# Grouped attention of layer one: transposes two rounds behind, value products as three rounded ones, ACT exchanges the query halves

## What is computed

```python
def _L0_attn_b_ref(hidden_states, Wq, Wkr, Wdk, Wupk, Wupv, Wo):
    q = (hidden_states @ Wq.T).reshape(bsz, q_len, N_HEADS, HEAD_DIM).transpose(0, 2, 1, 3)
    ...
    q = q * cos + _rotate_half(q) * sin
    k = k * cos + _rotate_half(k) * sin
    ...
    c_kv = hidden_states @ Wdk.T
    k_c = c_kv @ Wupk.T
    v = (c_kv @ Wupv.T).reshape(bsz, q_len, KV_HEADS, HEAD_DIM).transpose(0, 2, 1, 3)
    ...
    scores = jnp.einsum('bhqd,bhkd->bhqk', q, k) * scale
    scores = jnp.where(causal[None, None], scores, jnp.asarray(-1000000000.0, dt))
    attn = jax.nn.softmax(scores, axis=-1)
    out = jnp.einsum('bhqk,bhkd->bhqd', attn, v)
    return out.transpose(0, 2, 1, 3).reshape(bsz, q_len, N_HEADS * HEAD_DIM) @ Wo.T
```

## Time and profile before

| what | before |
|---|---|
| median of 3 runs | 2343.27 us |
| the profiled execution, its time | 2351.52 us |
| its span, first to last instruction | 2349.8 us |
| mean granted TensorE clock | 0.952 |
| PE, DVE, ACT, POOL busy | 90%, 60%, 46%, 36% |
| grouped attention, projections | 364 to 526 us |
| grouped attention, loop | 526 to 1276 us |

### The profile page before, as it was taken

The page is one execution under the profiler, slowest core; times in us unless marked ns, Lnnn a source line. Parts: engine busy times, 40 slices in busy tenths (PEclk is TensorE's granted clock), DMA queues, the critical chain, the costliest instruction groups (busy, mean ns, idle before and its releaser), DMA issues. The chain is left out here.

```text
span 2349.8 us, 33208 instructions
## 1 busy us (share of the span) xinstructions
PE 2125.6 (90%) x11408; PEld 1456.4 (62%) x11408; DVE 1406.4 (60%) x2597; ACT 1082.5 (46%) x2627; POOL 835.4 (36%) x1060
## 2 busy tenths in 40 slices
PE   5999988878999999999997879999999986899988
PEld 3333356656777777777765656777777674554457
DVE  5788464326656566556554636666666555657756
ACT  4677543214444444444443635555555433335553
POOL 0000101545344444444431035455555313246621
PEclk8999888989999999999999979999999987989999
DMA  3000022751011111111011144444333201543310
GB/s 112 1 1 1 4 90 84 153 128 41 25 53 37 36 54 32 41 54 32 23 41 36 62 103 108 108 108 105 88 98 78 61 23 58 160 91 68 72 33 37
DMA packets 113587, 149.48 MB, mean 64 GB/s; under 512 B 40127, under 2 KB 53567, under 8 KB 111246
## 3 DMA queue, kind: packets, MB, share of 16 engines
q1 hardware_dynamic: 65422, 109.08, 16.4%
q0 software_dynamic: 48000, 38.28, 7.1%
HBM read 86.39 MB, written 27.26 MB: 48 GB/s over the span
## 5 line engine op out<-in xcount | busy, mean ns | idle before, releaser
L1851 POOL TENSOR_TENSOR attn0b_probs<-attn0b_probs,attn0b_recip 128x128 f32<-128x128 f32 (+3 forms) x256 | 192.4, 772 | 223.4 <-DVE attn0b_recip L2090 223.3
L2482 POOL TENSOR_TENSOR attn1a_probs<-attn1a_probs,attn1a_recip 128x128 f32<-128x128 f32 (+3 forms) x256 | 178.9, 720 | 234.8 <-DVE attn1a_recip L2665 234.2
L2538 ACT ACTIVATE attn1a_probs<-attn1a_scores,attn1a_negmax 128x128 f32<-128x128 f32 (+3 forms) x256 | 132.7, 523 | 175.4 <-DVE attn1a_negmax L2651 174.2
L1957 ACT ACTIVATE attn0b_probs<-attn0b_scores,attn0b_negmax 128x128 f32<-128x128 f32 (+3 forms) x256 | 132.6, 523 | 150.0 <-DVE attn0b_negmax L2083 148.8
L1965 ACT ACTIVATE attn0b_probsT<-attn0b_turned 128x128 f32<-128x128 f32 (+3 forms) x128 | 56.0, 437 | 243.3 <-PE attn0b_turned L2231 242.9
L2244 PE MATMUL attn0b_out<-attn0b_probsT,attn0b_v_now 128*128 128x512 f32 x320 | 153.9, 612 | 11.4 <-DVE attn0b_probsT L2097 11.4
L1440 DVE TENSOR_REDUCE attn0a_negmax<-attn0a_by_query 128x2 f32<-128x1024 f32 x128 | 151.9, 1219 | 11.7 <-PE attn0a_by_query L1557 11.7
L2651 DVE TENSOR_REDUCE attn1a_negmax<-attn1a_scores 128x2 f32<-128x256 f32 (+3 forms) x128 | 105.4, 824 | 71.4 <-PE attn1a_scores L2840 71.4
L2083 DVE TENSOR_REDUCE attn0b_negmax<-attn0b_scores 128x2 f32<-128x256 f32 (+3 forms) x128 | 104.8, 819 | 46.9 <-PE attn0b_scores L2220 46.9
L37 PE MATMUL attn0b_aux<-attn0b_wo_hi,attn0b_oT_hi 128*128 128x512 f32 x256 | 125.6, 490 | 1.4 <-DVE attn0b_oT_lo L2101 1.4
L2852 PE MATMUL attn1a_turned<-ident_f,attn1a_probs 128*128 128x128 f32 x640 | 116.1, 280 | 8.7 <-DVE attn1a_probsT L2659 7.3
(11 more groups left out here) (507 smaller groups left out, 6121.2 us busy)
## 6 DMA issues: line engine op xcount, KB each, us to landing
pre<-in_b_o SPq DMA_DIRECT2D x16, 1024.0 KB, 5.3
attn1a_qT<-attn1a_stage SPq DMA_DIRECT2D x128, 128.0 KB, 2.4
attn1a_qT<-attn1a_stage SPq DMA_DIRECT2D x64, 256.0 KB, 3.8
pre<-in_b_q SPq DMA_DIRECT2D x8, 1024.0 KB, 6.1
pre<-in_b_kv SPq DMA_DIRECT2D x5, 1024.0 KB, 7.1
attn0b_vals<-attn0b_v_out SPq DMA_DIRECT2D x16, 256.0 KB, 5.0
attn0b_keys_hi<-attn0b_part_hi POOLq DMA_DIRECT2D x32, 128.0 KB, 4.9
attn0b_keys_lo<-attn0b_part_lo POOLq DMA_DIRECT2D x32, 128.0 KB, 7.6
```

The lines of the kernel that those rows point to most:

```text
L1851: pool.tensor_tensor(x, x, recip[:, r % 2, e:e + 1].broadcast_to([P, (qt + 1) * P]), ALU.mult).then_inc(s_scaled, 1)
L1957: act.activation(probs[:, r % 2, e, 0:width], scores[r % 2][:, e, 0:width], ACT.Exp, bias=negmax[:, r % 2, e:e + 1], accum_out=sums[:, r % ...
L2482: pool.tensor_tensor(x, x, recip[:, r % DEEP, e:e + 1].broadcast_to([P, (qt + 1) * P]), ALU.mult).then_inc(s_scaled, 1)
L2538: act.activation(probs[:, r % DEEP, e, 0:width], scores[r % 2][:, e, 0:width], ACT.Exp, bias=negmax[:, r % 2, e:e + 1], accum_out=sums[:, ...
```

## The change

- The probabilities, their sums and reciprocals have three buffers (`DEEP`). PE transposes a round two rounds after its scores: in the pass over `at` the first round of tile at-1 behind the query projection, and its second round at the end. The value product is that of tile at-2, the output product that of tile at-3.
- Both heads of a round are transposed and then leave together: `turned_hi` (ACT) writes the rounded part of both, `turned_lo` (DVE) the rest. The value product is three rounded matmuls per key block (`mm3`), with values in hi and lo.
- The projections therefore store the values in hi and lo: a subtraction (`value_lo`, DVE) and a store of twice the size; the loop loads both. In SP's order the second half of the values stands before the output weights of the next turn.
- Queries: ACT copies the two halves of the bank crosswise into `q_swap` (two buffers), DVE multiplies the bank by the cosine and `q_swap` by the sine table, whose halves are exchanged at loading: two multiplications for three. The bank is free for the output product after the cosine.
- Orders: on DVE `add_output` (of tile at-4) is first in a tile, `output_lo` and `query_lo` are last; on ACT `output_hi` and `query_hi` are last; on POOL both scalings of a tile and `add_rotated` are in the same pass. The query projection waits for the addition of tile at-4. The output weights are split at the end of the third tile of a turn.

```diff
...
-    FIRST, LAST = -LEAD, TILES_ALL + 1
+    DEEP = 3
+    FIRST, LAST = -LEAD, TILES_ALL + 3
...
-            v_out = take_sb("v_out", [P, 2, DIM])
-        q_cos, q_sin = n.sb("q_cos", [P, 2, SEQ]), n.sb("q_sin", [P, 2, SEQ])
+            v_out = take_sb("v_out", [P, 2, 2, DIM], F32R)
+        q_cos, q_swap = n.sb("q_cos", [P, 2, SEQ]), n.sb("q_swap", [P, 2, SEQ])
...
-        v_now = n.sb("v_now", [P, BATCH, QT, HD])
+        v_hi, v_lo = n.sb("v_hi", [P, BATCH, QT, HD], F32R), n.sb("v_lo", [P, BATCH, QT, HD], F32R)
...
-        probs = n.sb("probs", [P, 2, PAIRS, SEQ])
-        probsT = n.sb("probsT", [P, 2, QT, G, P])
+        probs = n.sb("probs", [P, DEEP, PAIRS, SEQ])
+        probsT_hi = [n.sb(f"probsT_hi{i}", [P, QT - 1 + i, G, P], F32R) for i in range(2)]
+        probsT_lo = [n.sb(f"probsT_lo{i}", [P, QT - 1 + i, G, P], F32R) for i in range(2)]
...
-        negmax, sums, recip = [n.sb(k, [P, 2, PAIRS]) for k in ("negmax", "sums", "recip")]
+        negmax = n.sb("negmax", [P, 2, PAIRS])
+        sums, recip = n.sb("sums", [P, DEEP, PAIRS]), n.sb("recip", [P, DEEP, PAIRS])
...
-        q_raw = n.sb("q_raw", [P, SEQ])
...
-                sp.wait_ge(s_v, at + 1)
-                sp.dma_start(vals[t, :, bass.ts(half, DIM)], v_out[:, at % 2, :]).then_inc(s_vals[at % 2], 16)
+                sp.wait_ge(s_vlo, at + 1)
+                sp.dma_start(vals[t, :, :, bass.ts(half, DIM)], v_out[:, at % 2, :, :].bitcast(F32)).then_inc(
+                    s_vals[at % 2], 16)
...
+                load_values(i, 1)
+                if i + 1 < TURNS:
...
-                load_values(i, 1)
...
         def _(pool):
...
             def add_rotated(c):
-                pool.wait_ge(s_rope, 3 * c + 3)
-                pool.tensor_tensor(q_cos[:, c % 2, :], q_cos[:, c % 2, :], q_sin[:, c % 2, :], ALU.add).then_inc(s_qadd, 1)
+                pool.wait_ge(s_rope, 2 * c + 2)
+                pool.tensor_tensor(q_cos[:, c % 2, :], q_cos[:, c % 2, :], q_swap[:, c % 2, :], ALU.add).then_inc(s_qadd, 1)
...
             def scale(r):
...
-                    x = probs[:, r % 2, e, 0:(qt + 1) * P]
-                    pool.tensor_tensor(x, x, recip[:, r % 2, e:e + 1].broadcast_to([P, (qt + 1) * P]),
+                    x = probs[:, r % DEEP, e, 0:(qt + 1) * P]
+                    pool.tensor_tensor(x, x, recip[:, r % DEEP, e:e + 1].broadcast_to([P, (qt + 1) * P]),
...
-                if 0 <= at <= TILES_ALL and 2 * at - 1 >= 0:
-                    scale(2 * at - 1)
-                if 1 <= c <= HEADS_ALL:
-                    add_rotated(c - 1)
...
+                if c < HEADS_ALL:
+                    add_rotated(c)
+                if 0 <= at < TILES_ALL:
+                    scale(2 * at + 1)
...
-                if r >= 2:
-                    act.wait_ge(s_turned, 2 * (r - 2) + e + 1)
-                    act.wait_ge(s_recip, r - 1)
-                act.activation(probs[:, r % 2, e, 0:width], scores[r % 2][:, e, 0:width], ACT.Exp,
-                               bias=negmax[:, r % 2, e:e + 1], accum_out=sums[:, r % 2, e:e + 1]).then_inc(s_exp, 1)
-            def copy_second(r):
+                if r >= DEEP:
+                    act.wait_ge(s_turned, r - DEEP + 1)
+                    act.wait_ge(s_recip, r - DEEP + 1)
+                act.activation(probs[:, r % DEEP, e, 0:width], scores[r % 2][:, e, 0:width], ACT.Exp,
+                               bias=negmax[:, r % 2, e:e + 1], accum_out=sums[:, r % DEEP, e:e + 1]).then_inc(s_exp, 1)
+            def turned_hi(r):
...
-                act.wait_ge(s_turned, 2 * r + 2)
+                act.wait_ge(s_turned, r + 1)
...
-                act.activation(probsT[:, at % 2, 0:qt + 1, 2 * p + 1, :], turned[:, 1, 0:qt + 1, :], ACT.Copy).then_inc(
-                    s_copied[1], 1)
+                act.activation(of_pair(probsT_hi, at, qt, p), turned[:, :, 0:qt + 1, :], ACT.Copy).then_inc(s_pthi, 1)
...
             def output_hi(at):
...
-            def query_out(c):
+            def swap_query(c):
...
-                if c >= 1:
-                    act.wait_ge(s_rope, 3 * c)
-                act.activation(q_raw[:, :], query_bank(c), ACT.Copy).then_inc(s_raw, 1)
+                if c >= 2:
+                    act.wait_ge(s_qadd, c - 1)
+                for into, of in ((slice(0, 64), slice(64, P)), (slice(64, P), slice(0, 64))):
+                    act.activation(q_swap[into, c % 2, :], query_bank(c)[of], ACT.Copy).then_inc(s_swap, 1)
...
             for at in range(FIRST, LAST + 1):
...
-                if at >= 2:
-                    output_hi(at - 2)
+                    for stored in s_keys:
+                        act.wait_ge(stored, 16 * 4 * 8)
+                if 0 <= 2 * at - 3 < ROUNDS:
+                    turned_hi(2 * at - 3)
...
-                    query_out(c)
-                if 1 <= at <= TILES_ALL:
-                    copy_second(2 * at - 1)
-                if 1 <= c <= HEADS_ALL:
-                    query_hi(c - 1)
+                    swap_query(c)
+                if 0 <= 2 * at - 2 < ROUNDS:
+                    turned_hi(2 * at - 2)
...
-                    copy_second(2 * at)
-                if at >= 0 and at % TILES == 1 and at // TILES < TURNS:
+                if 0 <= at - 2 < TILES_ALL:
+                    output_hi(at - 2)
+                if 1 <= c <= HEADS_ALL:
+                    query_hi(c - 1)
+                if at >= 0 and at % TILES == 2 and at // TILES < TURNS:
...
+            def value_lo(x):
+                dve.wait_ge(s_vhi, x + 1)
+                dve.tensor_tensor(v_out[:, x % 2, 1, :], proj[PROJ["V", x] % NB], v_out[:, x % 2, 0, :].bitcast(F32),
+                                  ALU.subtract).then_inc(s_vlo, 1)
...
+                    value_lo(7)
...
-                        dve.wait_ge(s_tables, 64)
+                        dve.wait_ge(s_tables, 80)
...
+                        value_lo(f[1] - 1)
...
+                elif f[1] >= 8:
+                    value_lo(f[1])
...
             def output_weights_lo(i, j):
...
-            def rotate(c):
-                dve.wait_ge(s_raw, c + 1)
+            def rotate_cos(c):
+                dve.wait_ge(s_swap, 2 * c + 2)
...
-                x = q_raw[:, :]
-                dve.tensor_tensor(q_cos[:, c % 2, :], x, cos_q[:, :], ALU.mult).then_inc(s_rope, 1)
-                for into, of in ((slice(0, 64), slice(64, P)), (slice(64, P), slice(0, 64))):
-                    dve.tensor_tensor(q_sin[into, c % 2, :], x[of], sin_q[of, :], ALU.mult).then_inc(s_rope, 1)
+                dve.tensor_tensor(q_cos[:, c % 2, :], query_bank(c), cos_q[:, :], ALU.mult).then_inc(s_rope, 1)
+            def rotate_sin(c):
+                dve.tensor_tensor(q_swap[:, c % 2, :], q_swap[:, c % 2, :], sin_q[:, :], ALU.mult).then_inc(s_rope, 1)
...
             def query_lo(c):
...
             def invert(r):
...
-                if r >= 2:
-                    dve.wait_ge(s_scaled, PAIRS * (r - 1))
-                dve.reciprocal(recip[:, r % 2, :], sums[:, r % 2, :]).then_inc(s_recip, 1)
-            def copy_first(r):
+                if r >= DEEP:
+                    dve.wait_ge(s_scaled, PAIRS * (r - DEEP + 1))
+                dve.reciprocal(recip[:, r % DEEP, :], sums[:, r % DEEP, :]).then_inc(s_recip, 1)
+            def turned_lo(r):
...
-                dve.wait_ge(s_turned, 2 * r + 1)
-                if at >= 2:
-                    dve.wait_ge(s_pv, at - 1)
-                dve.tensor_copy(probsT[:, at % 2, 0:qt + 1, 2 * p, :], turned[:, 0, 0:qt + 1, :]).then_inc(s_copied[0], 1)
+                dve.wait_ge(s_pthi, r + 1)
+                dve.tensor_tensor(of_pair(probsT_lo, at, qt, p), turned[:, :, 0:qt + 1, :],
+                                  of_pair(probsT_hi, at, qt, p).bitcast(F32), ALU.subtract).then_inc(s_ptlo, 1)
...
             def output_lo(at):
...
-                if at >= 2:
-                    output_lo(at - 2)
+                    for stored in s_keys:
+                        dve.wait_ge(stored, 16 * 4 * 8)
+                if 0 <= at - 4 < TILES_ALL:
+                    add_output(at - 4)
...
+                if 0 <= 2 * at - 3 < ROUNDS:
+                    turned_lo(2 * at - 3)
...
-                if 1 <= at <= TILES_ALL:
-                    copy_first(2 * at - 1)
+                if c < HEADS_ALL:
+                    rotate_cos(c)
...
-                    rotate(c)
+                    rotate_sin(c)
+                if 0 <= 2 * at - 2 < ROUNDS:
+                    turned_lo(2 * at - 2)
...
+                if 0 <= at - 2 < TILES_ALL:
+                    output_lo(at - 2)
...
-                if at >= 2:
-                    add_output(at - 2)
-                if 0 <= at < TILES_ALL:
-                    copy_first(2 * at)
-                if at >= 0 and at % TILES == 1 and at // TILES < TURNS:
+                if at >= 0 and at % TILES == 2 and at // TILES < TURNS:
...
+            def query_out_of_bank(c):
+                pe.wait_ge(s_rope, 2 * c + 1)
```

(44 more changed lines are left out.)

24 lines of the change are left out of this document (14 added, 10 removed).

## The result

The changed kernel takes 2353.8 us (median of 20 runs, 2348.06 to 2365.01). The kernel before, run beside it, takes 2348.8 us (20 runs, 2342.29 to 2355.12). The ratio is 1.0025, with a 95% interval of 1.0014 to 1.0036: slightly slower, where 2329 against 2343 had been forecast (ratio 0.994). The profiled executions have spans of 2349.8 and 2358.7 us. The two executions differ by 3.6 us before the block begins and by 3.5 us the other way behind it, in code that the change doesn't touch; so what is to be explained lies between the first matmul of the block and its last. One more thing to keep in mind: the profiled execution of the changed kernel took 2360.4 us, 6.6 above its median, at a mean granted clock of 0.938 where the median of its 20 runs is 0.941; that of the kernel before lies 2.7 us above its median.

A forecast was written before the change was run, and what follows sets the result against it. PE, busy 90% of the span, was taken as the bound, through its work and waits. Terms -27.5 + 7.5 + 5 - 3 + 4 = -14 us on the 2343.3 median gave 2329.3 us (forecast case 2315 to 2337, full range 2305 to 2353).

The forecast's parts named there:

- Part 1: Value product on PE: a key block falls from 0.86 to 0.69 us, 160 blocks, 27.5 us saved.
- R4: Rival: three matmuls cost three quarters of the old block, 0.645 us, saving 34.4 us; 2322 us, chance 0.08.
- Part 2: Middle of the attention: DVE stays at 386 us, ACT goes from 284 to about 345; neither becomes the bound.
- Part 3: Middle: later transposes remove 20 waits on POOL's scaling, about 20.5 us; new waits cost 28 us; +7.5 us.
- (a): A tile's first transposes wait for DVE's subtraction: 2.3 us, covered by 2.8 us of query projection, 0.5 to spare.
- (b): Query projection waits for the output addition queued behind DVE's four output-weight subtractions: 2.7 us, once per turn.
- (c): DVE's query part meets POOL's second scaling: 0.3 to 0.5 us in three tiles, 1.3 us a turn.
- 89 to 91.5: Sign: a turn of eight tiles takes 90.2 us, and the forecast is wrong outside this range in us.
- Part 4: Ends of the attention: last tiles' waits about 17 us against 12.0, +5; first queries sooner, -3 us.
- Part 5: Projections: doubled value stores cost 0 to 13 us, taken as 4; DVE's 16 subtractions lie in idle time.
- R2: Rival: gain used up, stores delay keys 13 us (+9), meetings cost 0.9 us each (+7); 2345 us, chance 0.20.

The follow-up runs named there:

- x2: Changed kernel, with PE doing 16 unused matmuls into a free bank before the late query projection in each turn's fourth tile; 2342.81 us, ratio 0.9979.
- x1: Changed kernel, with DVE's four output-weight subtractions moved from a turn's third tile to the middle of its fourth, behind the output addition; 2328.99 us, ratio 0.9912.
- x4: Changed kernel, with the output-weight subtractions spread over a turn's fourth tile and the output addition moved to the tile's end, before the query part; 2310.93 us, ratio 0.9844.
- b1: Kernel before, with DVE's value subtraction and the doubled value store added in the projections, old loop; 2356.43 us, ratio 1.0027.
- b3: Kernel before, with each value block stored twice (same copy) and no added DVE or ACT work; 2359.59 us, ratio 1.0047.
- b2: Kernel before, with DVE's 16 value subtractions alone added in the projections, bytes stored unchanged; 2354.7 us, ratio 1.0036.
- x7: Changed kernel, with POOL's scaling of the probabilities cut to one column per head, order and waits kept; 2330.28 us, ratio 0.9923.
- x5: x4, with DVE subtracting the transposed probabilities ahead of the maximum in the last five tiles; 2300.86 us, ratio 0.9798.
- x6: x5, with four buffers instead of two for the key parts in the projections; 2286.12 us, ratio 0.9732.

## Why the prediction was wrong

The forecast's sum was -14 us, and the two traces show +8.8 in the block (the medians +5.0). By the accounting above, against the forecast's terms, the step that failed most is one that the sum doesn't have: it takes PE's once-a-turn wait as its own length, and nothing for the clock behind it.

- **Part 1, the value product: right.** 0.69 us a block, as the rows show, and PE's work in the loop is 24 us less against 27.5. A part of it lies where the forecast didn't look: the output product behind the value product takes 2.73 us instead of 3.14, and the value product itself hardly gets shorter in the mean. The steps of the earlier trace rows ran into the output product, so the sum came out right. R4, three quarters of the old price, would have been 0.645 us a block, and didn't happen: the old form costs 0.86 us a block, 0.215 for a quarter of it, and the three rounded matmuls 0.23 each.
- **Part 2, what DVE and ACT get: right in kind, low in size.** The new subtraction costs what the reductions do. DVE has 408 us of the middle, where I had 386. 12 of these 22 us are the output weights, 29.3 us for 28 subtractions where 2.50 us for four would make 17.5. Another 12 are the query parts, 50.2 us for 56 where 0.68 us each would make 38. ACT has 359 (345). Neither is the bound.
- **Part 3, the waits: the sum near, by luck in part, and a consequence missing.** The waits on POOL's scaling went, and (a) held, with no such wait in the six whole turns. (b) was named with its place, and was 4.13 us instead of 2.7, in six turns and not seven. (c) was thought of as a wait of its own in three tiles, 1.3 us a turn; no such wait is in the trace. The meetings are there, and DVE's query part takes 0.90 us in the mean, but it costs PE something only in the third tile, and there POOL stretches subtractions of (b) as well, by its split of the query weights more than by the scaling: 1.9 us in all. (b) and (c) were forecast at 4.0 us a turn and came to 4.1, with the order priced too high and the meeting too low. I priced `wo_lo` by the 2.50 us of the earlier trace rows, where POOL happened to be idle, and checked the meeting with POOL for another instruction only.
- **The step that failed: the clock had no term.** The forecast had a wait of 2.7 us as 2.7 us. At each wait of 3.94 us the granted clock was 0.50 for 3.4 or 6.8 us, nearly all of it once PE went on, and PE did everything at half pace. Over the loop that is 21 us more than before by the accounting, about as much as those waits themselves. x2 shows this apart from the lateness: 11 us by the medians, 19 by the traces. In the whole turns x1 and x4 lose it along with the waits. This is the step that turned a forecast gain into a loss: -14 + 21 = +7. The turns show it too: those with 3.4 us of half clock took 90.5 and 90.8 us, those with 6.8 us 91.8 to 92.0, outside the 89 to 91.5 that I had set, and x2's without it 89.2. The forecast's terms, with 4.1 for (b) and (c), give 92.6 - 27.5/8 + 4.1 - 20.5/7 = 90.3, so the rest of the turn gained 1.1 us more than I had. Most of that is waits which the earlier trace rows doesn't list: in the kernel before, the transposes of a round's second head waited too, 0.34 or 0.13 us by the rows and 0.5 or 0.3 from start to start, 13 times between 560 and 1200 us, about 0.8 us a turn. The rest isn't traced. The clock alone doesn't make the forecast right, though: x2, with it back at 0.99 in the middle, still takes 2342.8 us, above the range.
- **Part 4, the ends: waits right, clock missing.** The last stretch's waits are 13.0, 2.4 and 0.9 us, 16.3 against the forecast's 17. Its granted clock of 0.89 over 80 us was again not in it (17 us at half clock, where the kernel before has none there). The beginning's gain of 3 us isn't seen: the first score of the changed kernel waits 11.2 us for its keys, so an earlier query would be of no use there.
- **Part 5, the stage before: right in kind, low in size.** 4 us forecast within 0 to 13; 8.7 in the trace and 6 to 11 by the ratios of b1 to b3. The failing step is that DVE's sixteen subtractions "lie in its idle time". DVE is idle for most of the stage, but the store and the bank wait for them, and b2 shows that they alone cost 5 us by the trace and 8 by the ratio. Which of the two it is that delays the stage stays open. The other part, the bytes, I had between 0 and 13 us; b3 shows 6 by the trace and 11 by the ratio.
- **A sum in the rivals.** R2 gives +7 us to meetings of 0.9 us. At 0.9 instead of 0.43 us in three tiles of seven turns it is +10, and R2 2348 us, which would still have been no change. R2's time came close, but not by its mechanism: most of the loss is in the clock, not in meetings of the query part.

By the accounting the misses are 21 us (clock), 5 (stage) and 3 (work), less 6 (waits, by the accounting +4 where +9.5 was forecast): 23 us between -14 and +9.

## What to carry to other kernels

Price a new wait of PE by what comes behind it as well: look in the trace whether idle pieces are followed by a lower granted clock, and split such a wait, or move what causes it, before anything else. An instruction's duration is good only for the company in which it was measured: before one of DVE with both inputs in SBUF is used in another place, look what POOL does there. Idle time of an engine covers a new step only if nobody waits for that step; with two buffers and a long landing, somebody does.

## What the runs showed of the hardware

- The granted clock of TensorE. In the changed kernel it fell to 0.50 (1.2 GHz) at each of the six waits of 3.94 us, between 1.1 us before PE went on and 1.1 us after. In x7 it fell in five turns of six behind waits of 2.06 us. In x1, with waits of 1.3 and 0.9 us, it didn't fall in the whole turns. Between the two lies no sharp line: in x4's tail it fell at waits of 1.89, 1.91 and 2.37 us and not at two of 1.92; the wait of 2.37 us, which x5 and x6 have at the same place, had a fall in x6 and none in x5. In the middle of the kernel before it fell once, for 3.4 us at 1043 us, behind waits of 1.10 and 0.34 us. At half clock a matmul of 512 columns comes every 0.43 us instead of 0.23, so that the query projection of twelve took 5.26 us. A turn with 3.4 us of half clock is 1.3 to 1.6 us longer than one without, a turn with 6.8 us 2.6 to 2.8.
- VectorE beside GpSimd: four subtractions with both inputs in SBUF take 2.50 us alone (x7), 4.16 or 4.17 beside two scalings (x1), and 4.18 to 4.22 beside a scaling and the split of a query weight (changed kernel, x2). It is single ones that are stretched, from 0.68 to between 1.31 and 1.78 us. The delay is mutual: the scaling of twice 512 columns takes 2.85 us at 651.21 in x1 and 2.04 us at 758.60 in the changed kernel.
- A key block of 512 columns costs 0.86 us as one fp32 matmul and 0.69 as three rounded ones, which follow each other every 0.23 us. The output product behind an fp32 one takes 3.14 us from its start, behind a rounded one 2.73: the 0.4 us are in its first step (880.74 to 881.37 in the kernel before, 0.63 us).
